# A chunked state-space scan: decay matrices over 64 by 64 tokens, state carried every 64 tokens

## The reference, cut to what matters

```
zxbcdt = xn @ in_proj_w                     # z 512, x 512, B 128, C 128, dt 32 columns
dt  = softplus(dt + dt_bias);  A = -exp(A_log)
xBC = silu(causal_conv1d(xBC))              # 4 taps
# 32 heads h of 16 channels p, state of 128 columns n
h_t = h_{t-1} * exp(dt_t * A) + (dt_t * x_t) outer B_t
y_t = h_t . C_t
y   = (y + D_skip * x) * silu(z);  y = y * rsqrt(mean(y^2) + eps) * rms_w;  out = y @ out_proj_w
```

## Time and profile before

| | us |
|---|---|
| median of 2 runs | 2903.9 |
| profiled execution, whole | 2915.6 |
| its span, first to last instruction | 2913.7 |
| PE busy | 2753.7 (95%) |
| DVE busy | 1776.3 (61%) |
| ACT busy | 1404.3 (48%) |
| POOL busy | 611.8 (21%) |

### The profile page before, as it was taken

How to read it: one execution, slowest core, us unless ns; L and a number is a source line. 1 busy time by engine, 2 the same in 40 slices (tenths; PEclk the granted TensorE clock), 3 DMA queues, 4 the chain that set the end, 5 groups by cost and what they waited for, 6 DMA issues and landing times. The chain is left out here.

```text
span 2913.7 us, 44479 instructions
## 1 busy us (share of the span) xinstructions
PE 2753.7 (95%) x17002; PEld 2075.9 (71%) x17002; DVE 1776.3 (61%) x3261; ACT 1404.3 (48%) x2418; POOL 611.8 (21%) x709
## 2 busy tenths in 40 slices
PE   5999999999988997999999999999999999999999
PEld 3555555555555554888887888888888887888887
DVE  6999999999999986577765333333333333333332
ACT  7777777777777774566553222222222222222221
POOL 1222222222222223000001222222222122222221
PEclk7999999999999998999999999999999999999999
DMA  2101010101010110542221000000000000000000
GB/s 79 46 22 46 22 38 23 38 22 39 22 38 22 38 46 23 165 149 68 69 68 31 15 17 1 15 17 15 17 15 17 15 1 17 15 17 15 17 15 8
DMA packets 104187, 99.31 MB, mean 34 GB/s; under 512 B 35998, under 2 KB 98718, under 8 KB 103206
## 3 DMA queue, kind: packets, MB, share of 16 engines
q1 hardware_dynamic: 102374, 96.41, 10.7%
q10 hardware_dynamic: 1600, 0.04, 0.0%
HBM read 68.00 MB, written 37.80 MB: 36 GB/s over the span
## 5 line engine op out<-in xcount | busy, mean ns | idle before, releaser
L1725 PE MATMUL fbank<-hid,fw 128*128 128x512 f32 x4096 | 962.3, 395 | 0.0
L1725 PEld LDWEIGHTS fbank<-hid,fw 128*128 128x128 f32 x4096 | 767.1, 188 | 186.0
L1873 DVE TENSOR_TENSOR hid<-fhf,hid 128x512 fp32r<-128x512 f32 x384 | 264.9, 690 | 703.3 <-POOL hid L1833 703.3
L1833 POOL TENSOR_SCALAR hid<-fhf 128x512 fp32r<-128x512 f32 x384 | 269.4, 701 | 1040.4 <-ACT fhf L1807 760.6
L1229 DVE SCALAR_TENSOR_TENSOR mh<-mh,gm 128x1024 f32<-128x1024 f32 x256 | 353.7, 1388 | 0.0
L916 ACT ACTIVATE mh<-ebank 128x512 f32<-128x512 f32 x512 | 293.9, 596 | 103.3 <-PE ebank L763 100.8
L1807 ACT ACTIVATE fhf<-fbank,sh1c 128x512 f32<-128x512 f32 x128 | 88.2, 689 | 383.7 <-PE fbank L1725 383.7
L1807 ACT ACTIVATE fhf<-fbank,sh2c 128x512 f32<-128x512 f32 x128 | 88.0, 688 | 382.5 <-PE fbank L1725 382.5
L763 PE MATMUL ebank<-cright,cleft 102*128 102x512 bf16 x512 | 210.6, 412 | 58.3 <-ACT mh L916 53.2
L776 PE MATMUL yin<-mh,xpad 128*32 128x128 f32 x4096 | 228.9, 298 | 28.4 <-DVE mh L1229 28.4
L750 PE MATMUL ebank<-ah,win 128*128 128x512 f32 x640 | 248.7, 432 | 5.2 <-ACT cin L949 5.2
(11 more groups left out here) (198 smaller groups left out, 4274.9 us busy)
## 6 DMA issues: line engine op xcount, KB each, us to landing
tok<-in_x SPq DMA_DIRECT2D x24, 512.0 KB, 4.9
tok<-x_d SPq DMA_DIRECT2D x17, 512.0 KB, 3.9
h_d<-in_h SPq DMA_DIRECT2D x16, 512.0 KB, 5.4
o_d<-tok SPq DMA_DIRECT2D x16, 512.0 KB, 2.9
fw<-h_d SPq DMA_DIRECT2D x2, 4096.0 KB, 16.0
out_x<-tok SPq DMA_DIRECT2D x16, 512.0 KB, 3.1
tok<-o_d SPq DMA_DIRECT2D x8, 512.0 KB, 3.9
mx<-in_x SPq DMA_DIRECT2D x8, 512.0 KB, 4.7
```

Source lines behind the costliest of these rows:

```text
L1725: mm = pe.matmul(bank[banks.slot(key)][:], w[:, k, m * P:(m + 1) * P].bitcast(dt), h[:, k, :].bitcast(dt), start=(k + n == 0), stop=(k == ...
L1833: pool.tensor_scalar(hid[i % 2][0][:, m, :], hf[j % 3][:], 1.0, 0.0, ALU.mult, ALU.add)\
L1873: dve.tensor_tensor(hid[i % 2][1][:, m, :], hf[j % 3][:], hid[i % 2][0][:, m, :].bitcast(F32), ALU.subtract).then_inc(c_lo.sem, 1)
```

## The change

The decay matrices cover 64 by 64 tokens. The first 64 tokens of a chunk stand in partitions 0 to 63, the second in 64 to 127, each half with its own matrix. So one bank holds the exponents of 8 heads (8 x 64 columns), and a chunk has 4 of them where it had 8. What the second half needs of the first now goes through the state: the state is brought forward every 64 tokens, in three buffers by turns, and `from_state` reads a state for each half. The running sum `cum` starts again at every 64th token (`keep_on`). The constant rows of `cleft` and `cright` change accordingly, and the six rows of `cum` parts of a chunk come in six DMAs of 64 columns instead of three of 128. All chunks now use a state, those at a sequence's start a zero one.

```
-ST_AT = 7
+ST_AT = (2, 7)
-STATE_AT = 8
+STATE_AT = (3, 8)
...
 def has_off(q):
-    return 0 <= q < CHUNKS and q % (NU * NC) > 0
+    return 0 <= q < CHUNKS
...
+def has_half(q, h):
+    return has_chunk(q) if h == 0 else has_state(q)
...
 def act_bank_order():
-        if has_chunk(q):
-            yield ("eb", q, i)
+        if i % 2 == 0 and has_chunk(q):
+            yield ("eb", q, i // 2)
...
 def dve_bank_order():
-        c = chunk_at(S, ST_AT)
-        if has_state(c):
-            yield ("st", c)
+        for h in range(2):
+            c = chunk_at(S, ST_AT[h])
+            if has_half(c, h):
+                yield ("st", c, h)
...
-    state = sb("state", [P, DI])
+    keep_on = sb("keep_on", [P, P])
+    state = [sb(f"state{j}", [P, DI]) for j in range(3)]
...
             def decay_right(q):
-                for j in range(3):
-                    sp.dma_start(cright[q % 2][96 + j:97 + j, :, :],
-                                 parts[q // NC % 2][NH * (q % NC):NH * (q % NC) + NH, j, :])\
-                        .then_inc(h_right.full(q), 16)
+                for h in range(2):
+                    for j in range(3):
+                        row = 97 + 3 * h + j
+                        sp.dma_start(cright[q % 2][row:row + 1, :, :],
+                                     parts[q // NC % 2][NH * (q % NC):NH * (q % NC) + NH, j, HQL * h:HQL * (h + 1)])\
+                            .then_inc(h_right.full(q), 16)
...
+            def intra(q, i, h):
+                key = (q, i)
+                if (i, h) == (0, 0):
                     released(pe, ("bt", q))
                     if q >= 2:
                         pe.wait_ge(c_yread.sem, c_yread.at(0, q - 1))
+                if h == 0:
+                    if i:
+                        pe.wait_ge(h_mh.free((q, i - 1)), h_mh.used(0, (q, i - 1)))
+                    pe.wait_ge(h_mh.full(key), h_mh.filled(0, key))
+                else:
+                    pe.wait_ge(c_first_half.sem, c_first_half.at(0, NG2 * q + i + 1))
+                s = slice(HQL * h, HQL * (h + 1))
+                for w in range(2):
+                    for j in range(G4):
+                        row = HD * 2 * j
+                        mm = pe.matmul(yin[q % 2][row:row + 2 * HD, i, s],
+                                       xpad[q % 2][s, G4 * i + j, w, :, :].rearrange("s w d -> s (w d)"),
+                                       mh[h_mh.slot(key)][s, 2 * j + w, :], start=(w == 0), stop=(w == 1),
+                                       tile_position=(HQL * h, row))
+                mm.then_inc(h_mh.free(key) if h else c_first_half.sem, 1)
...
             def from_state(q):
-                released(pe, ("st", q - 1))
+                released(pe, ("st", q, 0))
+                if has_state(q - 1):
+                    released(pe, ("st", q - 1, 1))
                 o = fresh(key)
                 for f in range(QI):
-                    mm = pe.matmul(o[:, f * P:(f + 1) * P], state[:, f * P:(f + 1) * P],
-                                   xc[q // NC % 2][:, QI + 1, tokens(q)], start=True, stop=True)
+                    for h in range(2):
+                        mm = pe.matmul(o[:, f * P + HQL * h:f * P + HQL * (h + 1)],
+                                       state_at(q, h)[:, f * P:(f + 1) * P],
+                                       xc[q // NC % 2][:, QI + 1, half_tokens(q, h)], start=True, stop=True)
...
+            def to_state(q, h):
+                key, s = ("st", q, h), slice(HQL * h, HQL * (h + 1))
+                pe.matmul(fresh(key)[:], bt[q % 2][s, :], xw[q % 2][s, :], start=True, stop=True,
+                          tile_position=(HQL * h, 0)).then_inc(full(key), 1)
...
             def masked(q, i):
                 released(dve, ("eb", q, i))
+                m_ = mh[h_mh.slot(key)]
+                dve.scalar_tensor_tensor(out=m_[:], in0=m_[:], scalar=1.0,
+                                         in1=gm[q % 2][:].unsqueeze(1).to_broadcast([P, G8, HQL]),
+                                         op0=ALU.min, op1=ALU.mult).then_inc(h_mh.full(key), 1)
...
+            def new_state(q, h):
+                key = ("st", q, h)
+                old = state_at(q, h)[:].rearrange("n (h d) -> n h d", d=HD)
+                new = state_at(q, h + 1)
+                if h == 0:
+                    released(dve, ("dtw", q // NC))
+                    if has_state(q - 1):
+                        released(dve, ("st", q - 1, 1))
+                    else:
+                        settled()
+                else:
+                    released(dve, ("st", q, 0))
+                mark(dve.tensor_tensor(new[:].rearrange("n (h d) -> n h d", d=HD), old,
+                                       dec[q // NC % 2][:, h, q % NC, :].unsqueeze(2).to_broadcast([P, NH, HD]),
+                                       ALU.mult))
                 made(dve, key)
+                settled()
+                dve.tensor_tensor(new[:], new[:], tile(key)[:], ALU.add).then_inc(free(key), 1)
```

More of the change, by code:

```diff
@@ L355, in mixer @@
     h_shsc = Handover(sem, "shsc", list(range(1, B)), 1, fills=16, both=False)
-    h_mh = Handover(sem, "mh", [(q, i) for q in chunks for i in range(NG // 2)], MH // 2, uses=2)
+    h_mh = Handover(sem, "mh", [(q, i) for q in chunks for i in range(NG2)], MH // 2)
     h_left = Handover(sem, "cleft", list(blocks), 2, fills=16 * 3 * NC, both=False)
-    h_right = Handover(sem, "cright", list(chunks), 2, fills=48, both=False)
+    h_right = Handover(sem, "cright", list(chunks), 2, fills=96, both=False)
     c_yread = Count(sem, "yin_read", 0)
@@ L772, in intra @@
                         pe.wait_ge(c_yread.sem, c_yread.at(0, q - 1))
-                pe.wait_ge(h_mh.full(key), h_mh.filled(0, key))
-                for j in range(G4):
-                    row = HD * 2 * j
-                    mm = pe.matmul(yin[q % 2][row:row + 2 * HD, i // 2, :],
-                                   xpad[q % 2][:, G4 * (i // 2) + j, i % 2, :, :].rearrange("s w d -> s (w d)"),
-                                   mh[h_mh.slot(key)][:, i % 2, j, :], start=(i % 2 == 0), stop=(i % 2 == 1),
-                                   tile_position=(0, row))
-                mm.then_inc(h_mh.free(key), 1)
+                if h == 0:
[13 more added lines that the diff above has]
+                mm.then_inc(h_mh.free(key) if h else c_first_half.sem, 1)
             def state_decay(q):
@@ L831, in b_by_token @@
                 o = fresh(key)
-                pe.matmul(o[:, 0:P], x_[:, QI, tokens(q)], x_[:, QI + 1, tokens(q)], start=True, stop=True)\
-                    .then_inc(full(key), 1)
+                for h in range(2):
+                    mm = pe.matmul(o[HQL * h:HQL * (h + 1), 0:HQL], x_[:, QI, half_tokens(q, h)],
+                                   x_[:, QI + 1, half_tokens(q, h)], start=True, stop=True, tile_position=(0, HQL * h))
+                mm.then_inc(full(key), 1)
                 key = ("bT", q)
@@ L871, in weights_by_token @@
                 pe.transpose(o[:, P:2 * P], wv[:], ident[:])
-                pe.matmul(o[:, 2 * P:3 * P], ones[:], dend[:], start=True, stop=True).then_inc(full(key), 1)
+                pe.matmul(o[:, 2 * P:4 * P], ones[:], dend[:].rearrange("p h t -> p (h t)"), start=True, stop=True)\
+                    .then_inc(full(key), 1)
             for S in range(FIRST, LAST):
@@ L887, in _ @@
                     from_state(c)
-                c = chunk_at(S, ST_AT)
-                if has_state(c):
-                    to_state(c)
+                for h in range(2):
+                    c = chunk_at(S, ST_AT[h])
+                    if has_half(c, h):
+                        to_state(c, h)
                 c = chunk_at(S, XT_AT)
@@ L1281, in _ @@
                 if i % 2 and has_chunk(q):
-                    masked(q, i)
-                c = chunk_at(S, STATE_AT)
-                if has_state(c):
-                    new_state(c)
+                    masked(q, i // 2)
+                for h in range(2):
+                    c = chunk_at(S, STATE_AT[h])
+                    if has_half(c, h):
+                        new_state(c, h)
+                    elif h and has_chunk(c):
+                        no_state(c)
                 c = chunk_at(S, ADD_AT)
```

170 lines of the change are left out of this document (82 added, 88 removed).

## The result

The changed kernel takes 3321.3 us (3320.8 and 3321.9) against 2903.9: 1.141 times as long, 95% interval 1.138 to 1.145. The forecast was 2990 with 3070 as its upper end: +417 us where +86 stood, so the direction alone was right.

What follows compares the result with a forecast made beforehand. The bound was taken to change inside a block between TensorE and VectorE. Links +3.7 and clock +2.4 us per block, over 15 blocks +91, with -3 for the last +88: 2903.9 + 88 = 2992, called 2990, range 2885 to 3070.

Steps and rivals of the forecast that it cites:

- The added wait: TensorE's first-half `to_state` waits for VectorE's second-half state update through a shared slot; second chunk 21.95 us against 19.02.
- The clock: TensorE at half clock after stops of 3 us at two places in a block: +2.4 us, ends 0 and +5.
- TensorE's work: Fewer `decay` products, costlier `from_state`, two `to_state`, `intra` unchanged: +1.0 us per chunk, ends +0.0 and +4.
- the small-product rival: TensorE's `intra` pays issue per small product, 0.5 to 0.6 us a step, not 0.35: some 3060 us, chance 0.2.
- the term for `intra`: On TensorE, sixteen instructions of 64 columns for eight of 128: no change, ends 0 and +0.3 us a step.
- VectorE's and ScalarE's work: VectorE's cheaper masks less an added state update, net -0.9 to -1.4 us per chunk; ScalarE some 2.4 us less.
- the wait for its gates: TensorE's 3.57 us wait while ScalarE does the gates and all `ebank` slots are full would have no cause left.
- The four links: Times between successive chunks' `x_by_token` products in a block: 19.2, 21.95, 18.4, 13.0 us; sum 72.5 against 68.8.
- it stands for some 3.5 us: TensorE's stop in a block's second chunk, ahead by 4.7 us less +1 us of its own work.
- The range: Whole-kernel time of 2885 to 3070 us, leaving out parts of the unbound and small-product cases, 2 in 10 together.

Runs made afterwards that it cites:

- e4: Kernel before, with one wait added on TensorE behind `from_state` (step 10) for VectorE's state update of step 8: 3037.5 us, 1.045 of before.
- e2: Kernel before, with the wait of e4 and another ahead of `to_state` (step 7) for VectorE's mask of step 3: 3115.7 us, 1.072 of before.
- e11b: Changed kernel with `to_state` and `intra` on all 128 rows and `from_state` in 128 columns (other results): 3194.2 us, 1.100 of before.
- e7: e1 with `from_state` in eight instructions of 128 columns from the chunk's first state alone (other results): 3039 us.
- e1: Changed kernel with VectorE-ring tiles in other banks, first-half state product in TensorE's step 4, its update in VectorE's step 5: 3116.2 us, 1.071 of before.
- e5: e1 with `to_state` made untiled over all 128 rows for either half (other results): 3115 us.
- e6: e1 with `intra`'s products over all 128 rows instead of 64 (other results): 3075 us.
- e9b: e1 with VectorE's first-half state update in its step 3 instead of 5: 3028.1 us, 1.042 of before.
- e12b: e9b with the three product edits of e11b (other results): 2935.8 us, 1.011 of before.

## Why the prediction was wrong, by its steps

**The added wait: right mechanism, half of it missed.** The prediction found that "the two `st` always share one slot", and drew only one of the two consequences. The first half's product waits for the second half's update; but the second half's product, in step 7, also waits for the first half's update, in VectorE's step 3. Since VectorE enters the chunk when TensorE ends its step 5, and has the readings of `yin` and x ahead of that update, this wait binds in six of the seven chunks of a sequence that have it, for 2.4 to 3.2 us (3.18 at 563.50), and the one that was foreseen in four of eight, for 1.1 to 2.4. e4 and e2 price their stand-ins in the old kernel at 130 and 78 us.

**The clock: the term that was mis-sized.** "+2.4 (ends 0 and +5)" us a block stood there; 14.5 was measured, or 13.9 with standing time counted once. Two errors are in it. I took half clock to come at two places; with both waits there are on average five stops of over 1 us in a block. And I took what a spell costs from the kernel before, with its products. e11b against the changed kernel shows that this doesn't carry over: same waits, 7.8 against 17.9 us of clock; and much of the loss lies where TensorE hardly stands (0.66 from 607.70 to 652.30). And a stop at half clock feeds itself: the late TensorE makes ScalarE and VectorE late (7.14, 4.51 and 6.88 us of waiting), and VectorE then has the next update late. That last part I argue from the timeline; no run isolates it.

**TensorE's work: right.** +4.0 us a block forecast, +3.4 measured in the rounded ledger and +4.0 in the unrounded one. `intra` takes 0.36 at full clock (556.12 to 556.48) for sixteen instructions, where eight took 0.35: the small-product rival is false. `from_state` takes 1.95 for its sixteen, where 1.8 was forecast, and e7, which undoes it, saves 2.6 of work in a block where 3.4 were put on it. A `to_state` takes 1.02 where it took 0.83, so two of them cost 1.2 more in a chunk; that is the upper end of the term, for which +1.0 was taken. The upper ends of the terms add up to some 4.5 a chunk, not to the +4 of the text, and the 0.66 of L852, on which the term for `intra` leans, is a duration; from start to start it is 0.59. Neither touched the forecast.

**VectorE's and ScalarE's work: less, as forecast, and no gain.** A mask takes 0.77 (page of the profile), and VectorE's busy time over 12 blocks goes from 766.0 to 742.7, 1.9 us a block; I had 3.6 to 5.6, since the cheaper masks were put between 0.55 and 0.69 and measured 1.37 - 0.77 = 0.60, the second update's scaling takes 0.83 us in the mean instead of 0.69, and the sequences' ends, half a one per block, gained a `yoff` and updates that I took at nothing. ScalarE's falls by 89 us, and the wait for its gates, 39.3 us in 11 stops of TensorE from 200 to 1000 us before, is gone as forecast. Whatever that gave, the stops and the clock took many times as much.

**The four links.** 19.2, 21.95, 18.4 and 13.0 were forecast; the windows have 25.6, 30.0, 21.1 and 19.0. The third is nearest, and not for the forecast's reason: its long stop, 2.69 us at 592.98, is the overlooked wait, and the foreseen one took 1.12. In the second, "it stands for some 3.5 us" at step 18 was 2.09; the stop at step 15 had come first and had made both engines late. From the end of the state's update to the next reading of `yin` 6.0 us stood, and it was 9.3 (577.30 to 586.59), with the clock at 0.67.

**The range.** It was built from mechanisms that each had a bound, but the clock's own bound was taken from one kernel with one long stop a block. No case had more stops than two, so nothing reached 3321. That the time rose, as forecast, is no success of the sum: of the 25.5 us that a block lost, 14.5 are in the term that had 2.4.

## What to carry to other kernels

When a tile is added to a ring, list each tile with the step in which its bank is asked for and the step of the other engine in which it is given back, for EVERY neighbour in the ring, and take the smallest distance; here the arrangement that came with one added tile was worth 10% of the time, and one edited line of the table and an assignment by name gave back 70% of the loss. Price TensorE's stops at more than their length: here 8.0 us of stops per block cost 4.8 us more in clock with the old products (e2), and 7.6 us of them 14.5 with the new ones. A ledger of idle time, lost clock and work per period shows in one step which of the three an edit moved.

## What the runs showed of the hardware

- A higher busy share of TensorE can go with a lower clock. In e1 TensorE was busy 927.8 of 991.0 us (94%) at 0.83 of its clock, in the kernel before 756.1 of 826.0 (92%) at 0.95. The Trainium skill, in TensorE: Matmul & The Clock Gate, under A second HAM failure mode: psum-queue depth-cycling, says of a kernel that cycles through PSUM banks that short, frequent idle times between groups of matmuls make the clock fall and come back over and over; e2 agrees (0.90 with the waits, 0.95 without).
- Four column groups at work take sixteen f32 instructions of 64 columns with their weight loads in 0.36 us (556.12 to 556.48), about the same as eight of 128 columns (0.35). TensorE: Matmul & The Clock Gate, in the Trainium skill, gives under Wait — 56ns, not 53.3ns? a floor of some 25 ns from start to start. An estimate from that page is 0.40 us for these sixteen alone; the measurement is below it, so here, with neighbours in different column groups, the floor didn't hold.
- An f32 product with 64 instead of 128 columns and 128 weight columns saved nothing: sixteen in 1.95 us (573.49), eight in 0.95.
- Executions of one kernel in this family agreed very unevenly: those of e1, e5 and e6 differ by 0.8 to 1.1%, those of e9b, e11b and e12b by 0.04% or less.
